# Keys' and queries' three bfloat16 parts written to DRAM and read back one by one

## What is computed

```
x = layernorm(x + recurrent_mixer(x))          # ternary projections, gated recurrence, small FFN
x = layernorm(x + cross_attention(x, context)) # 16 heads of 16 channels
x = layernorm(x + ffn(x))                      # 256 -> 1024 -> 1024 -> 256, weights +1/-1
```

```
Q = rope(x @ Wq.T + bq); K = rope(ctx @ Wk.T + bk); V = ctx @ Wv.T + bv
scores = Q K^T / 4, masked;  attn = softmax(scores);  out = (attn V) @ Wo.T + bo
```

## Time and profile before

| | |
|---|---|
| median of 3 runs | 880.45 us (879.28 to 882.05) |
| profiled execution | 882.22 us |
| its span | 880.3 us |
| mean granted TensorE clock | 0.993 |
| PE busy | 805.7 us, 92% of the span |
| DVE busy | 661.4 us, 75% |
| ACT busy | 550.9 us, 63% |
| POOL busy | 287.8 us, 33% |
| DMA | 57.45 MB, 32.0% of 16 engines' span |

### The profile page before, as it was taken

The page is one execution under the profiler, slowest core; times in us unless marked ns, Lnnn a source line. Parts: engine busy times, 40 slices in busy tenths (PEclk is TensorE's granted clock), DMA queues, the critical chain, the costliest instruction groups (busy, mean ns, idle before and its releaser), DMA issues.

```text
span 880.3 us, 17906 instructions
## 1 busy us (share of the span) xinstructions
PE 805.7 (92%) x6855; PEld 631.9 (72%) x6890; DVE 661.4 (75%) x1224; ACT 550.9 (63%) x917; POOL 287.8 (33%) x476
## 2 busy tenths in 40 slices
PE   2866688999999999999999999999999999999996
PEld 2443456787787878787877878787878778777775
DVE  6757678796969878887979798888879697856342
ACT  4754555849485766858494857668584948553522
POOL 7872124142414232242324142322424232320010
PEclk9999899999999999999999999999999999999999
DMA  9037031606060433316060614334160605142000
GB/s 300 2 67 119 25 55 44 91 13 110 25 123 26 85 61 67 80 38 110 13 110 25 117 31 85 61 63 83 38 109 13 110 25 103 21 85 39 1 13 24
DMA packets 52516, 57.45 MB, mean 65 GB/s; under 512 B 7856, under 2 KB 48848, under 8 KB 49360
## 3 DMA queue, kind: packets, MB, share of 16 engines
q1 hardware_dynamic: 52432, 56.31, 32.0%
HBM read 39.24 MB, written 16.79 MB: 64 GB/s over the span
## 4 chain that ended last, share of the span: by engine, by line
PE 70%; DVE 18%; POOL 4%; issue 3%; ACT 3%; DMA 1%; SPq 0%; ACTq 0%; DVEq 0%; POOLq 0%
PE bankC L1149 22%; PE bankA L1084 7%; PE slotB L1071 7%; PE bankA L1018 6%; PE bankA L953 6%; PE bankC L1133 6%; DVE nmax L1439 6%; PE slotB L1052 5%; PE bankC L1165 3%; DVE sg L1309 3%; PE bankA L934 2%; DVE bn L1390 2%; PE slotB L1095 1%; PE slotB L1103 1%; DVE h1l L1483 1%
## 5 line engine op out<-in xcount | busy, mean ns | idle before, releaser
L1149 PE MATMUL bankC<-h0h,w 128*128 128x256 f16 x1024 | 234.4, 273 | 0.5 <-DVE h0l L1483 0.5
L1149 PE MATMUL bankC<-h0l,w 128*128 128x256 f16 x1024 | 233.9, 272 | 0.0
L1439 DVE TENSOR_REDUCE nmax<-slotB 128x4 f32<-128x1024 f32 x128 | 155.1, 1215 | 28.0 <-PE slotB L1052 27.8
L825 ACT ACTIVATE pr<-slotB 128x1024 f32<-128x1024 f32 x128 | 127.7, 1029 | 19.5 <-PE slotB L1071 16.3
L1149 PEld LDWEIGHTS bankC<-h0h,w 128*128 128x128 f16 x1024 | 99.8, 97 | 17.1 <-issue 1.9
L1149 PEld LDWEIGHTS bankC<-h0l,w 128*128 128x128 f16 x1024 | 100.1, 98 | 15.0
L1052 PE MATMUL slotB<-k_st,q_st 97*128 97x256 bf16 x512 | 77.9, 276 | 10.5 <-issue 5.4
L604 POOL TENSOR_SCALAR rstd<-mv 128x2 f32<-128x2 f32 x48 | 9.2, 191 | 227.5 <-DVE mv L1393 227.4
L1071 PE MATMUL slotB<-q_st,k_st 99*128 99x256 bf16 x512 | 76.9, 273 | 4.1 <-ACT pr L825 2.5
L1483 DVE SCALAR_TENSOR_TENSOR h1l<-bankC,h1h 128x512 f16<-128x512 f32 x64 | 43.5, 679 | 40.2 <-ACT h1h L850 40.2
L1483 DVE SCALAR_TENSOR_TENSOR h0l<-bankC,h0h 128x512 f16<-128x512 f32 x64 | 43.9, 687 | 37.5 <-ACT h0h L850 37.2
(11 more groups left out here) (206 smaller groups left out, 1778.1 us busy)
## 6 DMA issues: line engine op xcount, KB each, us to landing
k_st<-scr SPq DMA_DIRECT2D x96, 128.0 KB, 4.5
q_st<-scr SPq DMA_DIRECT2D x96, 128.0 KB, 4.6
scr<-kpart SPq DMA_DIRECT2D x16, 384.0 KB, 2.8
scr<-qpart SPq DMA_DIRECT2D x16, 384.0 KB, 5.3
x<-in_x SPq DMA_DIRECT2D x16, 256.0 KB, 2.7
cT<-in_ctxT SPq DMA_DIRECT2D x16, 256.0 KB, 3.4
out<-x SPq DMA_DIRECT2D x16, 256.0 KB, 2.1
pr<-in_k SPq DMA_DIRECT2D x1, 1024.0 KB, 9.7
```

What stands on the lines that cost most here:

```text
L825: act.activation(pr[i % 2][:, c, :, :].rearrange("p h s -> p (h s)"), slotB[ringB.slot(g, name)][:, :], ACT.Exp, scale=DH ** -0.5).then_in ...
L1149: ins = pe.matmul(bankC[ringC.slot(g, name)][:, e * T:(e + 1) * T], w_1[:, i // 2, (2 * m + e) * P:(2 * m + e + 1) * P], (h0h, h0l)[i % 2] ...
L1439: dve.tensor_reduce(nmax[:, hg * HG * NT + n:(hg + 1) * HG * NT:NT], slotB[ringB.slot(g, name)][:, :].rearrange("p (h s) -> p h s", s=S), ...
```

## The change

The one semaphore for a put is replaced by three, one per part. put issues a DMA for each part as soon as that part is made. stack waits part by part and issues its reads in the order of parts, so that kget's mask row comes ahead of the first of these waits. The writers of kpart and qpart wait for the semaphore of their own part's earlier write. The tables of the order are the same.

```diff
-        qs_s, qr_s, qh_s, qparts = (count(n) for n in ("qs_s", "qr_s", "qh_s", "qparts"))
-        kout, qout = count("kout", 16), count("qout", 16)
+        qs_s, qr_s, qh_s, qp1_s, qparts = (count(n) for n in ("qs_s", "qr_s", "qh_s", "qp1_s", "qparts"))
+        kout, qout = ([count(f"{n}{i}", 16) for i in range(3)] for n in ("kout", "qout"))
...
                 if g >= 2:
                     sp.wait_ge(*(kst_in, qst_in)[n].at(g - 2))
-                sp.wait_ge(*made.at(g))
-                sp.dma_start(scr[g % 2, n].rearrange("i (c p) t -> p (i c) t", p=P),
-                             parts[:, :, :, :].rearrange("p i c t -> p (i c) t")).then_inc(gone.sem, 16)
+                for i in range(3):
+                    sp.wait_ge(*made[i].at(g))
+                    sp.dma_start(scr[g % 2, n, i].rearrange("(c p) t -> p c t", p=P), parts[:, i]).then_inc(gone[i].sem, 16)

             def kput(g):
-                put(g, 0, kpart, kparts, kout)
+                put(g, 0, kpart, (kh_s, kp1_s, kparts), kout)

             def qput(g):
-                put(g, 1, qpart, qparts, qout)
-
-            def stack(g, dst, n, which, arrived):
-                for s, i in enumerate(which):
-                    sp.dma_start(dst[DH * s:DH * (s + 1), :, :],
-                                 scr[g % 2, n, i].rearrange("(d h) t -> d h t", d=DH)).then_inc(arrived.sem, 16)
+                put(g, 1, qpart, (qh_s, qp1_s, qparts), qout)
+
+            def stack(g, dst, n, which, gone, arrived):
+                for i in range(3):
+                    sp.wait_ge(*gone[i].at(g))
+                    for s, part in enumerate(which):
+                        if part == i:
+                            sp.dma_start(dst[DH * s:DH * (s + 1), :, :],
+                                         scr[g % 2, n, i].rearrange("(d h) t -> d h t", d=DH)).then_inc(arrived.sem, 16)
...
-                sp.wait_ge(*kout.at(g))
                 sp.dma_start(k_st[g % 2][R_MASK:R_MASK + 1, :, :],
...
-                stack(g, k_st[g % 2], 0, PARTS_K, kst_in)
+                stack(g, k_st[g % 2], 0, PARTS_K, kout, kst_in)
...
-                sp.wait_ge(*qout.at(g))
-                stack(g, q_st[g % 2], 1, PARTS_Q, qst_in)
+                stack(g, q_st[g % 2], 1, PARTS_Q, qout, qst_in)
...
             def kparts_(g):
                 if g >= 1:
-                    pool.wait_ge(*kout.at(g - 1))
+                    pool.wait_ge(*kout[2].at(g - 1))
...
-                     "kp": lambda g: first_part(g, kt_s, kt1, kpart, kout, kh_s), "x1T": x1T_,
-                     "qp": lambda g: first_part(g, qr_s, qt1, qpart, qout, qh_s), "max": max_high,
+                     "kp": lambda g: first_part(g, kt_s, kt1, kpart, kout[0], kh_s), "x1T": x1T_,
+                     "qp": lambda g: first_part(g, qr_s, qt1, qpart, qout[0], qh_s), "max": max_high,
...
             def k_parts(g):
                 if g >= 1:
                     dve.wait_ge(*kparts.at(g - 1))
+                    dve.wait_ge(*kout[1].at(g - 1))
...
             def q_parts(g):
                 if g >= 1:
-                    dve.wait_ge(*qout.at(g - 1))
+                    dve.wait_ge(*qout[1].at(g - 1))
+                    dve.wait_ge(*qout[2].at(g - 1))
                 dve.wait_ge(*qh_s.at(g))
                 own.settle(dve.tensor_tensor(qrest[:, :, :], qt1[:, :, :], qpart[:, 0], ALU.subtract))
-                own.settle(dve.tensor_scalar(qpart[:, 1], qrest[:, :, :], 1.0, None, ALU.mult))
+                dve.tensor_scalar(qpart[:, 1], qrest[:, :, :], 1.0, None, ALU.mult).then_inc(qp1_s.sem, 1)
+                dve.wait_ge(*qp1_s.at(g))
                 dve.tensor_tensor(qpart[:, 2], qrest[:, :, :], qpart[:, 1], ALU.subtract).then_inc(qparts.sem, 1)
```

## The result

The changed kernel takes 875.94 us (median of 8 runs, 873.41 to 878.43) against 880.62 us of the kernel before (8 runs, 879.28 to 883.68). The ratio is 0.9943, with a 95% interval from 0.9926 to 0.9961. That is 4.7 us less. The profiled execution took 875.61 us, with a span of 873.6.

What follows compares the result with a forecast made beforehand. TensorE's queue was taken as the bound, so only its waits count: 3.9 us at score0 from sequence 2 on plus 1.2 for sequence 1, less 0.4 for scatter, 4.7 us; median from 880.45 to 875.8 us, range 873.4 to 880.0.

Steps and rivals of the forecast that it cites:

- The bound and the place: TensorE's queue bounds the kernel; its 5.4 us of waits at score0 are the last q_st read landing, passed on whole.
- The cost of the added issues and waits, 0: On SP and VectorE: 64 more DMA issues, 24 us, fall into existing waits, and passed waits cost next to nothing.
- B: Rival, slower: SP's issues become the bound, 0.76 us more before the first q read, 9.6 us, 890.1; chance 0.05.
- C: Rival, part-way: q_st is early, but TensorE's wait for x2 grows and takes half, 878.1 us; chance 0.07.
- Keys 1.1 us earlier: On SP's queue: mask row and part 0's reads follow the max rows at once, key reads start 1.1 us earlier.
- Queries 0.7 us by pipelining: At the query write: part 0's bytes finish before part 2's, so the first q read starts 0.7 us earlier.
- Shift 1.7 us: At score0: q_st lands about 1.7 us earlier, between 0.6 and 1.8, or 0 if the hole is misread.
- The bound by writes in series: At q_st: if three query writes land in series, the last 4.2 us after 453.0, 0.6 us of shift remains.
- Sum: Over all score0 waits: 3.9 us from sequence 2 on and 1.2 for sequence 1, 5.1; less 0.4, 4.7 us.
- the deduction of 0.4 for scatter: Taken off the 5.1 us gained at score0, for landings that scatter, leaving 4.7 us.
- The 1.2 counted for sequence 1: Gain at sequence 1's score0: 1.2 us of a 1.49 us wait, as the start's other chains are close behind.
- Rival A: No change: queries are late for the key reads ahead; each score0 wait shrinks by 0.2 us, 878.9; chance 0.20.

Runs made afterwards that it cites:

- delay experiments: Two extra 512 B DMAs before the q reads: kernel before 908.77 us; changed kernel, ahead of qget's waits 875.94 us, behind the first wait 885.29 us.
- keys alone: Changed kernel with the queries written whole and read as in the kernel before, only the keys in parts: 878.62 us, ratio 0.9966.
- the mask row alone: Kernel before with one line moved, the mask row's DMA ahead of the wait for the key write: 878.43 us, ratio 0.9987.
- the second profile: Changed kernel measured and profiled once more, nothing altered, as base for a later experiment: 875.36 us, ratio 0.9939.
- the queries alone: Changed kernel with the keys written whole and read as in the kernel before, only the queries in parts: 876.60 us, ratio 0.9933.

## Why the prediction was right, point by point

- **The bound and the place.** Right. All of the gain is at score0, and the waits ahead of it are gone. The delay experiments show that the landing of the last q_st read was what they waited for, and that a wait is passed on whole. Even a little more than whole: the 49.26 us with the wait of 1.09 stand 1.17 above the floor of 48.09; the 48.18 that the prediction set beside them held a wait of 0.04 itself.
- **The cost of the added issues and waits, 0.** Right: two further issues ahead of the q reads (in front of SP's wait) cost nothing. DVE's busy time is 660.7 us against 661.4, and the wait for x2 is 6.9 against 7.0. Rivals B and C fall. But SP's cover is only in front of that wait: behind it, two issues cost 10 us even in the changed kernel, and 27 in the kernel before. They don't test B's price of 9.6 us, for they are another DMA: 0.57 us an issue instead of 0.38, with longer reads behind.
- **Keys 1.1 us earlier.** Right at the keys (mask row 1.3, key reads 1.2 us), wrong in what arrives: 0.6 at the q reads on average (keys alone 0.59; the mask row alone 0.54). The step that failed is "the first read so starts 1.1 us + 0.7 us before 453.06". It took the query write as something that lands a fixed time behind the key reads. With the keys alone that holds in six of twelve sequences (1.10 us earlier); in the other six the write landed 1.8 to 2.1 us behind the last key read instead of 0.7 to 1.0, and nothing arrived. Which transfer or wait makes the second group is open.
- **Queries 0.7 us by pipelining.** Right: 0.74 alone, 0.81 beside the keys. The size is that of the landings: part 0's comes 0.61 us before part 2's on average, 0.4 to 0.7 in single sequences, while their issues are 1.69 us apart. So the landings follow the bytes, which still move together when the key reads are through, and not the issues.
- **Shift 1.7 us.** Measured 1.43 on average, and 1.67 in the second profile. In four sequences (3, 5, 10, 13) the first read came only at 5.1 to 5.8, with 0.2 to 0.9 us to spare at score0; no wait came of it.
- **The bound by writes in series.** The 128 KB writes of the keys land in 1.8 us each, and three of them cost the key reads no time. Those of the queries overlap, with landings some 0.3 us one behind the other. A sum in series isn't seen. The Trainium skill (DMA: Bandwidth & Descriptors, Anatomy of one DMA) gives the fixed 2.0 us for DMAs that GpSimd issues. The writes here go out on SP, and their 1.8 us, bytes included, lie just under that figure.
- **Sum.** 4.7 us were forecast and 4.7 measured in the medians. In the profiled executions it is 6.6 of span. The waits from sequence 2 on gave 4.9 and not 3.9, 1.0 more than their rows list, and the deduction of 0.4 for scatter wasn't needed. The 1.2 counted for sequence 1 came as 1.55, but two kernels that write the queries whole have no wait there either: the prediction took what one execution showed for every one. Another 0.4 is in the start, which the change hardly touches. So the sum of 4.7 came out with one term too small and one that not every execution has, and that the medians fit it so closely is partly luck; their interval leaves 3.4 to 6.5 us.
- **Rival A** falls: the whole change and the queries alone each lie clear of 878.9, and the hole behind the write could be shortened.

## What to carry to other kernels

Where the trace calls a wait "issue", add the time to landing to the start of the last DMA that the instruction needs: if it comes out some 0.1 us before its start in every sequence that waits, the DMA is the likely releaser, and a delay put in ahead of that DMA shows it. Slack is worth only what it takes away in waits: the queries' part alone gave the whole gain with a third of the slack, and the other half of the change bought safety. Slack has to be there in every period; the keys' part alone had more of it on average and left four waits. Before sending one DMA as three, look whether the issuing queue stands in front of a wait or behind it, for the same two issues cost nothing in the one place and 10 to 27 us in the other.

## What the runs showed that was not expected

- Two DMAs of 512 B from DRAM to DRAM, put ahead of six large reads, took 0.57 us of issue each and made the reads 0.3 us longer on average from first issue to last landing (8.18 against 7.84; in single sequences up to 1.5). In the changed kernel it is 8.32 against 7.96 and 8.17.
- The single 384 KB write of sequence 1's queries, with no key reads queued ahead, moved its bytes within about 1.5 us and landed 4.5 us after its issue; the one of sequence 0 landed in 2.7, and the same data in three parts in 1.8 us each. In sequence 1 it took 4.4 us with the keys alone, but 2.7 with the mask row alone and with the delay added, so it isn't tied to the sequence. Elsewhere, too, single writes landed 1.4 to 2.0 us later than their like (the keys' of sequence 14 in the kernel before: 4.2 against 2.8). The cause stays open.
- The time from part 2's subtraction to the first q read is in two groups in the changed kernel, about 4.4 us (eight sequences of 2 to 13) and 5.1 to 5.8 (3, 5, 10, 13). Sequence 3 is in the late group in every kernel with the keys in parts; the others change from kernel to kernel. In the kernel before, the query writes of sequences 2 and 7 are late in the same way, 1.8 and 2.0 us behind the last key read against 0.6 to 1.1 in the others, and their waits of 0.60 and 1.09 us come of it. Which transfer makes the difference is open.
